# Four of sixteen context sums moved from VectorE to ScalarE and GpSimd in a cross-attention and mixture-of-experts kernel

## The reference

```python
x = x + tanh(g_xattn[0]) * align(ctx_1024, layernorm(x))
h = layernorm(x)
w, sel = top_k(h @ gate_w.T, 2)          # softmax over the two
x = x + tanh(g_ffn[0]) * sum_over_the_two(w * (h @ expert_w[sel].T))
```

## Time and profile before

| what | us |
|---|---|
| median of three runs | 566.42 |
| lowest and highest | 566.21, 568.12 |
| the profiled execution | 567.43 |
| its span, first to last instruction | 565.7 |
| TensorE busy | 429.7 (76%) |
| VectorE busy | 462.7 (82%) |
| ScalarE busy | 240.3 (42%) |
| GpSimd busy | 220.5 (39%) |

### The profile page before, as it was taken

How to read it: one execution, slowest core, us unless ns; L and a number is a source line. 1 busy time by engine, 2 the same in 40 slices (tenths; PEclk the granted TensorE clock), 3 DMA queues, 4 the chain that set the end, 5 groups by cost and what they waited for, 6 DMA issues and landing times. The chain is left out here.

```text
span 565.7 us, 8020 instructions
## 1 busy us (share of the span) xinstructions
PE 429.7 (76%) x1826; PEld 249.9 (44%) x1837; DVE 462.7 (82%) x1972; ACT 240.3 (42%) x462; POOL 220.5 (39%) x215
## 2 busy tenths in 40 slices
PE   7999943647613230468789979999999999999991
PEld 7999832425412220134344634444444444444441
DVE  6868889999998888589989839999977997789900
ACT  5457789874565520299557212222222222222220
POOL 4570203000000000000336446768676868688654
PEclk9999978676756665579899979999999999999996
DMA  8966244452007500177699998679797979799776
GB/s 282 339 220 208 78 117 112 118 163 49 1 0 265 181 2 0 49 299 254 208 288 251 250 314 181 119 136 164 133 165 137 161 131 165 131 167 164 115 93 76
DMA packets 61387, 88.88 MB, mean 157 GB/s; under 512 B 24933, under 2 KB 25189, under 8 KB 61181
## 3 DMA queue, kind: packets, MB, share of 16 engines
q0 software_dynamic: 16048, 37.31, 36.6%
q1 hardware_dynamic: 38701, 42.64, 23.2%
q10 hardware_dynamic: 6592, 8.42, 4.9%
HBM read 48.92 MB, written 39.43 MB: 156 GB/s over the span
## 5 line engine op out<-in xcount | busy, mean ns | idle before, releaser
L2086 PE MATMUL psum<-big,tokens 128*128 x304 | 132.6, 592 | 0.0
L763 POOL DMA_INDIRECT stage<-x_rows,row_ids x57 | 56.1, 985 | 195.0 <-DVE row_ids L1241 175.8
L2086 PE MATMUL psum<-big,work 128*128 x256 | 115.6, 603 | 0.0
L1399 DVE STREAM_TRANSPOSE tokens<-stage 32x256 f32<-32x256 f32 x192 | 83.7, 436 | 15.5 <-DMA stage<-x_rows,row_ids 13.0
L1399 DVE STREAM_TRANSPOSE work<-stage 32x256 f32<-32x256 f32 x192 | 83.7, 436 | 8.6 <-DMA stage<-x_rows,row_ids 6.0
L2086 PEld LDWEIGHTS psum<-big,tokens 128*128 128x128 f32 x304 | 57.1, 190 | 68.9 <-issue 68.9
L783 POOL DMA_INDIRECT out_dram<-tokens,row_ids x36 | 58.2, 1617 | 53.4 <-SPq L606 18.1
L2086 PEld LDWEIGHTS psum<-big,work 128*128 128x128 f32 x256 | 48.5, 194 | 56.1 <-issue 56.1
L1728 ACT ACTIVATE tokens<-psum,tile_shares 128x512 f32<-128x512 f32 x36 | 24.6, 687 | 94.0 <-PE psum L2086 71.7
L783 POOL DMA_INDIRECT out_dram<-prow,row_ids x34 | 55.3, 1627 | 22.3 <-issue 7.7
L1728 ACT ACTIVATE prow<-psum,tile_shares 128x512 f32<-128x512 f32 x34 | 23.4, 687 | 92.5 <-PE psum L2086 59.7
(11 more groups left out here) (398 smaller groups left out, 697.5 us busy)
## 6 DMA issues: line engine op xcount, KB each, us to landing
tokens<-in_x_dram SPq DMA_DIRECT2D x16, 1024.0 KB, 12.3
stage<-in_L_ffn_expert_w_dram ACTq DMA_DIRECT2D x8, 1024.0 KB, 5.4
out_dram<-tokens SPq DMA_DIRECT2D x8, 1024.0 KB, 14.1
x_rows<-tokens SPq DMA_DIRECT2D x7, 1024.0 KB, 7.3
tokens<-dist_rows SPq DMA_DIRECT2D x52, 64.0 KB, 2.1
dist_rows<-work SPq DMA_DIRECT2D x16, 160.0 KB, 2.0
dist_rows<-prow SPq DMA_DIRECT2D x5, 256.0 KB, 9.8
x_rows<-tokens SPq DMA_DIRECT2D x4, 256.0 KB, 4.8
```

What stands on the lines that cost most here:

```text
L763: pool.indirect_dma_start(out=tiles_in(n)[:, 0, :], out_offset=None, in_=x1_d[0:T, :] if n < FA else x1_d[:, :], in_offset=bass.IndirectOf ...
L1399: ins = v.transpose(to[:, :, :, NB * g:NB * (g + 1)], got[:, :, :, a, :])
L2086: ins = nc.tensor.matmul(psum[:, UP + n % UP, :], tileT(n, c), expT[:, bass.ds(own, 1), c, :].rearrange("p o d -> p (o d)"), start=(c == 0 ...
```

## The change

VectorE no longer adds the sums of tiles 12 to 15. ScalarE copies each out of PSUM, scaled (`lift`), into one of two rows of `work`, and GpSimd adds that row to x. The four lifts stand in front of squares(5) to squares(8); a third and a fourth lift wait until the first and second addition are done with their row. With two engines finishing rows, `x1_done` replaces the wait on `s_x1`: it waits for VectorE's own count and, past tile 12, for GpSimd's. On VectorE place_first stands straight behind count_first_tiles, and scales(0) moves behind the sums of tiles 18 and 19. Two semaphores set in the beginning (`eps` and a column of ones) become one.

```diff
--- before.py
+++ after.py
@@ -322,8 +322,7 @@
         s_cc = sem("ctx_centred")
         s_aam = sem("ctx_norms")
         s_aab = sem("ctx_norms_turned")
-        s_eps = sem("eps_set")
-        s_one = sem("one_set")
+        s_eps = sem("eps_and_one_set")
         s_edge = sem("wave_border_set")
         s_aTp = sem("ctx_transposed")
         s_aT = sem("ctxT_copied")
@@ -388,6 +387,7 @@
         s_m2 = sem("x1_means")
         s_e = sem("aligned")
         s_x1 = sem("x1")
+        s_lift = sem("context_lifted")
         s_sq = sem("x1_squares")
         s_sd2 = sem("x1_std")
         s_rs = sem("x1_rstd")
@@ -472,6 +472,12 @@
             where, at = blockT(n)
             return where[:, at, c * P:(c + 1) * P]
 
+        def x1_done(eng, k):
+            own = min(k, TB - POOLED) + max(0, k - TB)
+            eng.wait_ge(s_x1, own)
+            if k > TB - POOLED:
+                eng.wait_ge(s_pc, CHAINED + min(k, TB) - (TB - POOLED))
+
         def tile_of(t):
             return x[:, bass.ds(t, 1), :].rearrange("p o c -> p (o c)")
 
@@ -488,6 +494,9 @@
         right = [max(q - 1, 0) for q in range(NB)]
 
         CONSTS = 16
+        CHAINED = 8
+        POOLED = 4
+        LIFTS = 5
         WARM = 10
         TR = (0, 1, 2, 3)
         AT = (4, 5, 6, 7)
@@ -572,7 +581,7 @@
                 sp.dma_start(x[:, GT * g:GT * g + GT, :], x_v[g]).then_inc(s_x[g], 16)
 
             def rows_out(g, k0, k1):
-                sp.wait_ge(s_x1, GT * g + k1)
+                x1_done(sp, GT * g + k1)
                 sp.dma_start(x1_d[g * GW + k0 * P:g * GW + k1 * P, 0:C].rearrange("(k p) c -> p k c", p=P),
                              x[:, GT * g + k0:GT * g + k1, :]).then_inc(s_rows[g], 16)
 
@@ -734,6 +743,12 @@
                 pool.wait_ge(s_do[i], 16 * GB)
             nc.gpsimd.memset(stopr[:, :, :], 0.0).then_inc(s_tabk, 1)
 
+            for k in range(POOLED):
+                t = TB - POOLED + k
+                pool.wait_ge(s_lift, k + 1)
+                pool.wait_ge(s_x[t // GT], 32)
+                nc.gpsimd.tensor_tensor(x[:, t, :], work[:, 2 + k % 2, :], x[:, t, :], ALU.add).then_inc(s_pc, 1)
+
             def gather(n):
                 if n == 0:
                     pool.wait_ge(s_ids, 1)
@@ -821,7 +836,7 @@
                 v.wait_ge(s_vc, chain[0])
 
             v.memset(eps[:, :], EPS).then_inc(s_eps, 1)
-            v.memset(onecol[:, :], 1.0).then_inc(s_one, 1)
+            v.memset(onecol[:, :], 1.0).then_inc(s_eps, 1)
             def borders():
                 link(v.memset(edge, BIG))
                 for q in range(2 * B):
@@ -1416,8 +1431,6 @@
             for t in range(8, 12):
                 add_context(t)
             count_first_tiles()
-            for t in range(12, TB):
-                add_context(t)
             place_first()
             lay_first_lanes()
             lay_first_numbers()
@@ -1427,9 +1440,9 @@
             add_context(17)
             pick(0, 1)
             logits(1)
-            scales(0)
             for t in (18, 19):
                 add_context(t)
+            scales(0)
             pick(1, 0)
             pick(1, 1)
             leave_first()
@@ -1525,7 +1538,7 @@
                 to = dst[0:HP, u % 2, :]
                 nc.scalar.activation(to[:, ::-1] if h else to, dsq[0:HP, u % 2, :], ACT.Sqrt).then_inc(s_dd, 1)
 
-            act.wait_ge(s_eps, 1)
+            act.wait_ge(s_eps, 2)
             nc.scalar.activation(best[:, 0:1], eps[:, :], ACT.Sqrt).then_inc(s_eps, 1)
             gate_centred()
             gate_turned()
@@ -1661,7 +1674,6 @@
             def cells_second():
 
                 act.wait_ge(s_span, 2)
-                act.wait_ge(s_one, 1)
                 act.wait_ge(s_late, 8)
                 n = 0
                 for half in range(2):
@@ -1680,7 +1692,7 @@
             cells_second()
 
             def squares(t):
-                act.wait_ge(s_x1, t + 1)
+                x1_done(act, t + 1)
                 if t:
                     act.wait_ge(s_sq, t)
                 if t % TB == 0:
@@ -1699,7 +1711,17 @@
                 ts = slice(b * TB, (b + 1) * TB)
                 nc.scalar.activation(sc[:, 1, ts], sc[:, 0, ts], ACT.Exp).then_inc(s_gte, 1)
 
+            def lift(t):
+
+                act.wait_ge(s_e, t + 1)
+                k = t - (TB - POOLED)
+                if k >= 2:
+                    act.wait_ge(s_pc, CHAINED + k - 1)
+                nc.scalar.mul(work[:, 2 + k % 2, :], psum[:, bank(t), :], tgates[:, 0:1]).then_inc(s_lift, 1)
+
             for t in range(TB):
+                if LIFTS <= t < LIFTS + POOLED:
+                    lift(TB - POOLED + t - LIFTS)
                 squares(t)
             root(0)
             nc.scalar.activation(gates[:, 0:1], eps[:, :], ACT.Exp)
@@ -1958,9 +1980,9 @@
             def align(t):
                 b = t // TB
                 if AR <= t < TB:
-                    pe.wait_ge(s_x1, t - AR + 1)
+                    x1_done(pe, t - AR + 1)
                 if t >= TB:
-                    pe.wait_ge(s_x1, TB + 1 + BEFORE[t - TB][0] if BEFORE[t - TB] else TB)
+                    x1_done(pe, TB + 1 + BEFORE[t - TB][0] if BEFORE[t - TB] else TB)
                 if bank(t) == 6:
                     pe.wait_ge(s_outside, 1)
                 if t == TB + 7:
@@ -2003,7 +2025,7 @@
             def invert_first_shares():
 
                 pe.wait_ge(s_shareh, 1)
-                pe.wait_ge(s_x1, TB + 6)
+                x1_done(pe, TB + 6)
                 for i in range(TB):
                     ins = nc.tensor.matmul(psum[:, 5, 0:PARTS * FA], lanes_first[:, :, i],
                                            parts_first[:, i, :, :].rearrange("p s j -> p (s j)"),
@@ -2081,7 +2103,7 @@
                 if n >= UP:
                     pe.wait_ge(s_ye, n - UP + 1)
                 else:
-                    pe.wait_ge(s_x1, TB + LATE.index(UP + n) + 1)
+                    x1_done(pe, TB + LATE.index(UP + n) + 1)
                 for c in range(CH):
                     ins = nc.tensor.matmul(psum[:, UP + n % UP, :], tileT(n, c),
                                            expT[:, bass.ds(own, 1), c, :].rearrange("p o d -> p (o d)"),
```

## The result

The changed kernel takes 571.47 us in the median against 566.42, a ratio of 1.0089 (95% interval 1.0069 to 1.0109): 5.0 us slower. On another occasion (the first experiment) it measured 1.0046 (1.0011 to 1.0082). All ratios here are estimates over many executions, not quotients of two medians: the medians of that second occasion, 570.26 and 566.56, would give 1.0065. The executions spread widely, from 567.95 to 574.44 us, and one more, in the chip's occasional slower state, took 577.78 and is left out of the ratio. The profiled one, 567.95 with a span of 566.2, is the fastest of them: it is good for mechanisms and understates the cost.

What follows compares the result with a forecast made beforehand. VectorE's stream to the ids at 269.22 us sets when TensorE's busy tail starts. Ids +3.6 and second low stretch +0.5 gave +4.1 on 566.42, 570.5 us; range 566.8 to 573.2, the forecast's own 568.4 to 571.8.

Steps and rivals of the forecast that it cites:

- The late sixteenth sum: TensorE's align(16) waits for all sixteen sums: start at 266.4 instead of 262.97 us, TensorE idle 4.0 us.
- The lifts' pitch: ScalarE's four lifts, one square between each, start at 259.9, 261.4, 262.9 and 264.4 us; the last ends at 265.1.
- The additions: GpSimd's four additions take 1.17 us each, bounds 1.05 and 2.1, each ending before the next lift.
- The last addition: GpSimd's fourth addition runs from about 265.2 to 266.35 us, set by ScalarE's chain.
- VectorE's lists: Without four sums on VectorE, the numbers are ready at 265.3 instead of 267.97 us, 2.6 us gained; VectorE then idles.
- rival C: VectorE and GpSimd block each other in SBUF, delaying the third addition: +0.8, in all +4.9 us, 571.3; chance 0.14.
- The ids: VectorE's first ids, read at 269.22 us before, come 3.6 us later; bounds +2.0 and +4.7.
- the low clock's share: TensorE's clock falls after its 4.0 us stop; 3.4 us of low clock raises the ids' delay from +2.0 to +3.6.
- The second low stretch: TensorE idles some 2.3 us before the first turn and the first product may run slowly: 0.5 us, bounds 0 and 1.3.
- scales(0): Behind two sums on VectorE it comes 1.3 us later, nearly covered by the count's 1.1 wait: nothing, bounds 0 and 0.2.
- Absorbed later: Delay lost before the second list's first gather, at most about 1 us by that path; 566.4 to 567.4 us, chance 0.12.

Runs made afterwards that it cites:

- the first experiment: The changed kernel measured once more, unaltered, for a second profile; ratio 1.0046 to the kernel before, median 570.26 us.
- write_only: The changed kernel with GpSimd's four additions replaced by constant fillings that read nothing, leaving four sums out of x; ratio to before 1.0071.
- fill_16: The changed kernel with 14 unread matmuls of 512 columns in front of align(16), where TensorE stood idle; ratio to before 1.0006, median 566.96 us.
- after: The changed kernel itself against the kernel before, first measurement and profile; median 571.47 us, ratio 1.0089.
- after_again: The changed kernel measured and profiled a second time, nothing altered; ratio to before 1.0046, median 570.26 us.
- scales_back: The changed kernel with scales(0) put back in front of the sums of tiles 18 and 19; ratio to before 1.0063.

## Why the prediction came out as it did

The direction and the path were right; the time is 1.0 us above the forecast of 570.5, inside its own range. The second measurement lies below it, by 1.5 us if the ratio is taken and 0.2 if the median of 570.26. That the first came so near is in part luck: the ids moved 0.8 us less than forecast, and behind them 2.2 us were lost where 0.5 were put.

*The late sixteenth sum.* Right: align(16) started at 265.31 and TensorE had stood idle 3.2 us. The lifts' pitch was mis-sized: they follow 1.28 us apart, not 1.5, since a lift starts 0.72 us behind the start of the square in front of it, where another square starts after 0.90. The additions take 1.27 us instead of 1.17, just what the lifts' pitch is, so both chains bind; with write_only's fillings GpSimd waits 0.17 us for each next lift, and the starts still lie 1.28 us apart. The last addition ended 1.2 us earlier than forecast, or 0.8 counted from the first sum.

*VectorE's lists.* Wrong in the step that left them at 265.3 us, as idle slack, and in rival C's remark that VectorE's delay would be hidden. The four locked operations put the numbers at 269.03, where four sums at full clock would have ended too (265.31 and the 3.6 us that they take in fill_16). So two legs lie side by side: take the lock away (write_only) and the slow sums hold the ids at 22.9; take the low clock away (fill_16) and the numbers hold them at 22.1. The lock of C was real, but it struck VectorE's small operations and not, as priced, the third addition. Its price is 0.9 us at the ids where the clock is held (22.1 and 21.2 us), and nothing that can be told in the time (1.0006 and 1.0001). The rule the prediction cited from the Trainium skill (SBUF — State Buffer, Who interferes with whom) is what the traces show: the two-input operations take 1.12 to 1.36 us beside reading additions, 0.17 to 0.29 beside fillings that only write. The remark that the trace before has no such pair was wrong: between 90.4 and 92.7 us four GpSimd subtractions of 18 elements per partition, 0.22 to 0.29 us each, lie beside VectorE's TENSOR_TENSOR operations of 64, which take 0.19 to 0.24 as elsewhere. So short a neighbour told nothing for C.

*The ids.* Forecast +3.6, measured +2.8 and +2.7: the low clock's share there was mis-sized, for behind slower numbers it costs at most the difference between the legs, 1.0 us by fill_16.

*The second low stretch.* Right. It came in both profiles: products of 5.88 and 5.26 us behind stops of 2.25 and 2.03 us. The price was paid where VectorE waits for the first shares: 1.0 us more in the first profile, and place_choices is done 3.4 us late behind ids that are 2.8 late. In the second profile it is done 2.6 us late, no more than the ids. The 0.5 taken lies between.

*scales(0).* Put at nothing, "nearly covered"; alone it measured 0.43%, in the changed kernel nothing that can be told (1.0063 with it put back). The step weighed the 1.3 us against the wait in front of the count. It left out that the product can be at low clock, 2.4 us longer, so that the wait is no longer there and the first shares, with 0.8 us of VectorE's waiting already, come late. What part the move has in this stays open, since in its profile the clock had fallen before it.

*What brings 2.8 to 5.0.* The second measurement, 1.0046 or 2.6 us, asks for nothing beyond the ids; the first does. Filling in front of align(16) recovers some 0.4% (1.0046 to 1.0006) where its ids gain is 1.0 us. For the rest, the low stretches behind later stops differ between executions: the end minus the second list's first turn is 237.2 us before, and 235.5, 235.6, 237.8 and 238.0 in the four unfilled profiles with the same late sixteenth sum (after, after_again, write_only, scales_back). That these differences make up the median's excess was argued from single profiles, and is not shown.

*Absorbed later* (D): its limit held. Before, the gather waited for rows landed 1.4 us after the second list's ids began; after, it followed these ids within 0.6 us (324.15, and 324.74 above), and 0.8 us came back by that. In after_again the gather waited for rows again, 1.7 us, and nothing came back.

## What to carry to other kernels

Before moving work off the busiest engine, look at what else the moved result releases: here the sum was needed by a queue with 1.4 us of slack, and came 2.8 us later. Beside GpSimd additions that read SBUF, four of VectorE's small operations took about as long as an addition each, so such additions belong where VectorE has no chain of small operations that others wait for. Where TensorE had to stop for some microseconds, 32 unread matmuls in two of its gaps were worth 0.5%, more than any reordering tried here.

## What the runs showed of the hardware that was not expected

VectorE's one-input operation of 8 elements was shut out as well: L1215 of the changed kernel took 1.23 us beside a GpSimd addition, and two of its like 1.25 and 1.24 in after_again. Beside a mere filling its like took 0.35 and 0.49 us, while the two-input ones were left alone (0.17 and 0.29). So the additions, which read and write, held up both kinds, and the fillings, which only write, the one-input scalar ones, though not each of them.

A stop of the same kind does not always cost the clock: behind 3.22 us of idleness the sums ran at 0.50 in the first profile, and behind 2.66 us at full clock in the second; behind the 2.25 and 2.03 us in front of the first turn it fell in both. In scales_back, where the product follows the turn 2.0 us later instead of 2.7 and 2.8, it stayed up behind 2.05 us.
